# Linear attention slots: values' products earlier, features ahead of residuals and turns, scatter and sum of looked-up rows on GpSimd

## The chip, the cores and the metric

One core of a Trainium2 chip. The metric is the device time of one execution in microseconds (us). The engines are TensorE (PE; PEld is its weight load), VectorE (DVE), ScalarE (ACT), GpSimd (POOL) and SyncE (SP), each with its own instruction stream; they meet at semaphores. SP and GpSimd also issue the DMAs that are spoken of here.

## The reference, cut to what matters

A block of six residual layers on 4 x 512 tokens of width 512. The first three are of interest, the kernel weaves them:

```python
x = x + 0.5 * L0_ffn(layernorm(x))      # looked-up spline rows: route, look up, scatter, sum
x = x + L0_attn(layernorm(x))           # linear attention with sine features
x = x + 0.5 * L0_ffn(layernorm(x))
# then two Hadamard feed-forwards around a differential attention
# L0_attn:
q, k = rotate(h @ Wq.T + bq), rotate(h @ Wk.T + bk); v = h @ Wv.T + bv
qp = concat(sin(p), cos(p)) / sqrt(F),  p = (q / |q|) @ R.T      # kp likewise, of k
kv = einsum('bhsf,bhsd->bsfd', kp, v)   # per token, summed over heads
out = einsum('bhsf,bsfd->bhsd', qp, kv);  return out @ Wo.T + bo
# L0_ffn, after routing a token to one of 64 tiles of 8 columns:
delta = (b + s * x_local) * output_scale[tile]
out = zeros.at[n, cols of tile].set(delta);  return x + out
```

The scatter is computed as one-hot (64 tiles) times delta (8 numbers), both broadcast to 512 columns, and then added to x.

## The kernel before

The tokens are cut into four chunks of 512 rows (4 tiles of 128). Products are made of pairs of f16 (high and low parts), three matmuls per contraction block. After the weights are set up, the kernel runs five **slots**, i = -1 to 3 (b_tensor L1290, b_scalar L1474, b_pool L1577, b_sync L1631, b_vector L1658). In slot i three chunks are in work at once (b_roles): `now` = i has its scores, weighted sums, output product and residual; `new` = i + 1 gets projections, rotation, lengths, features and values; `look` = i + 2 gets its looked-up rows, its norm and its turned rows; `back` = i - 1 is routed for the third layer. There is no planner: the order on each engine is the program's order, written by hand.

A slot has a **loop** of 17 steps (y = 0 to 16) and a **tail**. In the loop TensorE makes score(y) (L1310) and weighted(y - 1) (L1323), with the mask by the vector engine between (L1667). At fixed steps it also makes the projections of `new` (QK_AT), the lengths' sums (L1342), the turned features (L1352, steps 14 and 15) and the look-up of `look` (L1267). The vector engine does the rotation (L1685), the look-up's arithmetic, at step 12 the scaling of the rows (L1847), at 13 the scatter (L1853), at 14 the refine of the inverse root of the lengths (L1697 to L1699), at 14 also the sum (L1113), at 15 the statistics of the next norm (L2079). GpSimd does the sums and squares of the rotation (L1585, L1589). weighted(y) waits for mask(y), and mask(y) stands behind whatever the vector engine has before it.

The tail makes, for `new`, spread(a) (L1362, a copy of it on ScalarE at L1498), angle(z) (L1709, L1713, L1714), the Sin and its high part (L1504, L1507) and the low part (L1721), for z = 0 to 5. Between these stand the values' products (L1195 with 256 columns, evicted at L1740), the norm's root and rows of `look` (L2097, L2121), its turned rows (L1904, L1912, L1919), and the output products of `now` with their residuals (L1729), then, in slots 1 and 2, the routing (L447 to L479).

The features have to be laid anew, heads and features over the partitions, for the next slot's scores. They go through DRAM: SP stores the high parts pair by pair (L1602) and loads them again (L1609), GpSimd does the same for the low parts (b_low_spread, the same two lines), each waiting for a pair's store to land before its load. SP also stores the values (L1648) and loads them in eight DMAs (L1653), between the second and third pair. score(0) of the next slot waits for all of the features and for the values to be evicted; weighted(0) waits for the eight loads. The buffers of features and values are single.

Of the kernel before, what the change touches and what calls it, by code (L numbers as in the profile page):

```python
# [88 lines left out]
b_reduced b_feat b_f_hi b_f_lo b_hi_out b_lo_out b_ks b_ks2 b_ksg b_qs b_qs2 b_s b_mask b_pv b_ot_hi b_ot_lo b_out b_res b_bo  # L89
# [1132 lines left out]
QK_AT = (0, 1, 3, 4, 6, 7)  # L1222
TURN_AT = (14, 15)
# [4 lines left out]
LOOK_SCALE, LOOK_SCATTER, LOOK_ADD, LOOK_NORM = 12, 13, 14, 15  # L1228
# [61 lines left out]
def b_tensor(k, pe, i):  # L1290
# [54 lines left out]
    def turned(a):  # L1345
        pe.wait_ge(s["b_rot"], 6 * new + 2 * a + 2)
        if a == 0:
            pe.wait_ge(s["b_rope"], 6 * (new + 1))
        else:
            need(pe, s["b_y"], 3 * new + a - 1)  # L1350
# [13 lines left out]
    def output(u):  # L1364
# [4 lines left out]
        if u < 2 and new is not None:  # L1369
            pe.wait_ge(s["b_v_in"], TPC * new + u + 3)  # L1370
# [6 lines left out]
    def value(u):  # L1377
        if new is None:
            return
        if u >= 2:  # L1380
            pe.wait_ge(s["b_v_in"], TPC * new + u - 1)
        cols = slice(u * P, (u + 1) * P)
        pairs_product(pe, k.ps[:, ROWS_OUT[u % 2], 0:256], [of(h, cols) for h in ht],
                      [of(w, slice(768, 1024)) for w in w0]).then_inc(s["b_v_done"], 1)

    for y in range(PAIRS + 1):
        if now is not None:
            if y < PAIRS:
                score(y)
            if y:  # L1390
                weighted(y - 1)
        if new is not None:
            if y in QK_AT:
                project(QK_AT.index(y))
            if y in LENGTH_AT:
                length(LENGTH_AT.index(y))
            if y in TURN_AT:
# [76 lines left out]
def b_scalar(k, e, i):  # L1474
# [46 lines left out]
    for y in range(PAIRS + 1):  # L1521
        if now is not None and y and y % 4 == 0:
            sums(y // 4 - 1)
        if new is not None and y == SPREAD_AT + 1:
            inverse()
        if look is not None and y == LOOK_START + 1:
            apply_scalar(k, e, look, 1, LOOK_BANK)
        if look is not None and y == LOOK_NORM + 1:
            use_log(e)
            norm_root_scalar(k, e, look)  # L1530
# [15 lines left out]
    spread(0)  # L1546
    feature(0)
    if look is not None:
        norm_write_scalar(k, e, look, look, k.h, range(2), s["n_h"])
    spread(1)  # L1550
    feature(1)
    if look is not None:
        norm_write_scalar(k, e, look, look, k.h, range(2, TPC), s["n_h"])
    feature(2)
    spread(2)
    feature(3)
    if look is not None:
        turn_scalar(k, e, look, 0, NEXT_TURN[0])
    feature(4)
    if look is not None:  # L1560
        turn_scalar(k, e, look, 1, NEXT_TURN[1])
    feature(5)
    keys(0)
    if look is not None:
        turn_scalar(k, e, look, 2, NEXT_TURN[2])
# [1422 lines left out]
```

## Time and profile before

| | |
|---|---|
| runs of the kernel (us) | 2229.55, 2238.29, 2240.41; median 2238.29 |
| profiled execution (us) | 2230.0, of which 2228.2 from first to last instruction |
| busy: PE, DVE, ACT, POOL | 87%, 57%, 32%, 11% |
| mean granted TensorE clock | 0.932 of full speed |
| the five slots | about 237 to 636 us |
| first score of slots 0 to 3 | 317.98, 411.12, 509.13, 594.68 us |
| first Sin of slots -1 to 2 | 286.17, 379.31, 477.01, 563.23 us |

The page cuts the span into 40 slices of 55.7 us; the slots are slices 5 to 12. Matmul idleness is worth reading by what ended it, since an idle stretch of an engine that nothing waits for costs nothing.

### The profile page before, as it was taken

The page shows a single profiled execution, that of the slowest core. Times are in us where ns is not written, and L with a number is a line of the kernel's source. Part 1 is how long each engine was busy: PE and PEld are TensorE (multiplying, and loading weights), DVE is VectorE, ACT ScalarE, POOL GpSimd, SP SyncE. Part 2 cuts the span into 40 slices and gives each one's busy share as a digit, 9 for nine tenths or more (in the row PEclk, how much of TensorE's full clock was granted, in tenths as well). Part 3 has the DMA queues.
Part 4 walks back from the last instruction along what each step waited for, and adds up shares of the span by engine and source line. Part 5 has one row for each costly group of instructions (what it writes and reads, how often), then busy time and mean ns, then how long its engine had stood idle before and what let it go on. Part 6 is the DMA issues. An engine that isn't in the chain of part 4 may idle for free.

```text
span 2228.2 us, 28781 instructions
## 1 busy us (share of the span) xinstructions
PE 1943.6 (87%) x11782; PEld 925.8 (42%) x11782; DVE 1259.0 (57%) x2312; ACT 720.2 (32%) x1109; POOL 246.1 (11%) x200
## 2 busy tenths in 40 slices
PE   3876668787664999899999999999999999999999
PEld 2443334343342444344444444444444444444444
DVE  5776658578756564636674456635664456533332
ACT  3553133343322133222353224522353224412211
POOL 1830212213100000000000100000000100000000
PEclk7887879889776999999999999999999999999999
DMA  7223240330412123211120211111020211132321
GB/s 258 97 62 110 87 90 20 71 73 18 90 76 96 67 105 114 94 67 40 37 76 30 72 52 49 57 57 39 29 76 29 76 48 58 48 112 97 123 96 66
DMA packets 92457, 164.93 MB, mean 74 GB/s; under 512 B 44134, under 2 KB 55718, under 8 KB 87718
## 3 DMA queue, kind: packets, MB, share of 16 engines
q1 hardware_dynamic: 89446, 156.79, 21.8%
q0 software_dynamic: 2880, 6.31, 1.2%
q8 instruction: 93, 1.52, 0.3%
q14 instruction: 38, 0.31, 0.0%
HBM read 137.89 MB, written 25.17 MB: 73 GB/s over the span
## 4 chain that ended last, share of the span: by engine, by line
PE 50%; DVE 4%; ACT 2%; issue 1%; ACTq 0%; DVEq 0%
PE ps L1195 27%; PE ps L1989 12%; PE ps L2503 2%; PE ps L2522 1%; DVE arena L2667 1%; PE ps L2499 1%; PE ps L2505 1%; PE ps L2449 1%; PE ps L2540 1%; PE ps L2524 1%; PE ps L2526 1%; PE ps L2529 1%; PE ps L2531 1%; PE ps L2446 1%; DVE arena L2044 0%
## 5 line engine op out<-in xcount | busy, mean ns | idle before, releaser
L1195 PE MATMUL ps<-arena 128*128 128x512 f16 (+1 forms) x4512 | 1010.1, 379 | 22.9 <-DVE arena L2044 12.8
L1195 PEld LDWEIGHTS ps<-arena 128*128 128x128 f16 x4512 | 434.0, 98 | 529.9 <-issue 28.4
L1989 PE MATMUL ps<-arena 128*128 128x512 f16 x1536 | 343.8, 379 | 12.5 <-DVE arena L2072 9.3
L1989 PEld LDWEIGHTS ps<-arena 128*128 128x128 f16 x1536 | 146.6, 97 | 185.8 <-DVE arena L2072 12.1
L2044 DVE SCALAR_TENSOR_TENSOR arena<-arena,ps 128x512 f32<-128x512 f32 x128 | 87.8, 686 | 208.5 <-ACT arena L2011 207.9
L2011 ACT ACTIVATE arena<-ps,arena 128x512 f32<-128x512 f32 x128 | 87.7, 685 | 358.6 <-PE ps L1195 358.4
L2596 ACT ACTIVATE arena<-ps 128x1024 f32<-128x1024 f32 (+3 forms) x128 | 90.2, 705 | 254.4 <-PE ps L2505 254.4
L2701 DVE CAST arena<-arena 128x1024 f16<-128x1024 f32 (+3 forms) x128 | 66.2, 517 | 150.6 <-ACT arena L2596 148.6
L2667 DVE TENSOR_REDUCE arena<-ps 128x2 f32<-128x256 f32 (+3 forms) x128 | 99.5, 819 | 65.1 <-PE ps L2449 65.1
L2072 DVE SCALAR_TENSOR_TENSOR arena<-ps,arena 128x512 f32<-128x512 f32 x64 | 44.0, 687 | 134.5 <-PE ps L1989 134.3
L2053 DVE SCALAR_TENSOR_TENSOR arena<-ps,arena 128x512 f32<-128x512 f32 x128 | 95.7, 748 | 39.2 <-PE ps L1195 39.1
L2703 DVE TENSOR_TENSOR arena<-arena 128x1024 f16<-128x1024 f32 (+3 forms) x128 | 111.4, 870 | 4.4
L2647 POOL TENSOR_TENSOR arena<-arena 128x512 f16<-128x512 f32 x32 | 37.1, 1160 | 624.1 <-ACT arena L2574 624.1
L2035 DVE TENSOR_TENSOR arena<-arena 128x512 f16<-128x512 f32 x128 | 90.8, 710 | 4.0 <-ACT arena L2003 4.0
L1667 DVE TENSOR_TENSOR arena<-ps,arena 128x256 f32<-128x256 f32 x128 | 47.4, 416 | 68.8 <-PE ps L1310 68.4
L2003 ACT ACTIVATE arena<-arena 128x512 f16<-128x512 f32 x128 | 79.6, 622 | 17.5 <-DVE arena L2053 17.5
L2651 POOL TENSOR_TENSOR arena<-arena 128x512 f32<-128x512 f32 x16 | 19.0, 1187 | 581.6 <-DVE arena L2714 581.6
L741 PE MATMUL ps<-arena 128*128 128x128 f32 x240 | 45.3, 332 | 37.3 <-DVE arena L979 18.6
L2571 ACT ACTIVATE arena<-ps 128x512 f32<-128x512 f32 x32 | 19.1, 597 | 166.7 <-PE ps L1195 166.7
L2503 PE MATMUL ps<-arena 32*128 32x512 f16 (+3 forms) x768 | 72.8, 293 | 0.0
L1323 PE MATMUL ps<-arena 128*32 128x64 f32 x1024 | 41.9, 294 | 33.2 <-DVE arena L1667 32.8
L1904 PE MATMUL ps<-arena 128*128 128x128 f32 x192 | 30.1, 303 | 43.9 <-ACT arena L2121 40.2
(270 smaller groups left out, 2342.4 us busy)
## 6 DMA issues: line engine op xcount, KB each, us to landing
arena<-wug_dram SPq DMA_DIRECT2D x128, 512.0 KB, 3.3
arena<-wd_hi_dram SPq DMA_DIRECT2D x16, 1024.0 KB, 5.0
arena<-wd_lo_dram SPq DMA_DIRECT2D x16, 1024.0 KB, 7.2
wug_dram<-arena SPq DMA_DIRECT2D x4, 2048.0 KB, 16.1
arena<-feat_dram SPq DMA_DIRECT2D x24, 256.0 KB, 4.7
arena<-_attn_hidden_states_dram SPq DMA_DIRECT2D x4, 1024.0 KB, 15.9
arena<-in_L_ffn_W_up_dram SPq DMA_DIRECT2D x8, 512.0 KB
arena<-in_L_ffn_W_down_dram SPq DMA_DIRECT2D x4, 1024.0 KB, 7.2
```

The costliest lines, as they stand in the source:

```text
L1195: ins = pe.matmul(out, left[a](c), right[b](c), start=(at == 0), stop=(at == 3 * n - 1))
L1989: ins = pe.matmul(k.ps[:, bank, :], act[x][:, slot, cols], wd[y][:, f, :], start=(f == 0 and m == 0), stop=(f == 7 and m == 2))
L2003: e.activation(k.act_hi[:, g % ACT_SLOTS, :], k.prod[:, g % 2, :], ACT.Copy).then_inc(s["f_hi"], 1)
L2011: e.activation(k.th[:, g % 2, :], k.ps[:, GATE_BANK, :], ACT.Tanh, scale=k.wscale[:, FB + a:FB + a + 1])\
L2035: e.tensor_tensor(k.act_lo[:, g % ACT_SLOTS, :], k.prod[:, g % 2, :], k.act_hi[:, g % ACT_SLOTS, :], ALU.subtract)\
L2044: e.scalar_tensor_tensor(out=th, in0=th, scalar=1.0, in1=k.ps[:, GATE_BANK, :], op0=ALU.add, op1=ALU.mult)\
L2053: e.scalar_tensor_tensor(out=k.prod[:, g % 2, :], in0=k.ps[:, UP_HALF_BANK, :], scalar=k.wscale[:, a:a + 1], in1=th, op0=ALU.mult, op1=ALU ...
L2503: pe.matmul(k.ps[:, bank, queries], x[rows, 4 + b, keys], y[rows, b, queries], start=False, stop=False)
L2596: e.activation(k.p32[:, t % 2, :, queries], k.ps[:, 0:2, queries], ACT.Exp, scale=SCORE).then_inc(s["c_exp"], 1)
L2667: e.tensor_reduce(k.mx[:, u, 4 * b + 2 * j:4 * b + 2 * j + 2], k.ps[:, bank:bank + 2, 0:(u + 1) * P], AXX, ALU.max).then_inc(s["c_max"], 1)
L2701: e.tensor_copy(k.p_hi[:, t % 2, :, queries], k.p32[:, t % 2, :, queries]).then_inc(s["c_p_hi"], 1)
L2703: e.tensor_tensor(k.p_lo[:, t % 2, :, queries], k.p32[:, t % 2, :, queries], k.p_hi[:, t % 2, :, queries], ALU.subtract).then_inc(s["c_p_l ...
```

## The change

Five edits, all in the slots:

- the values' products and evictions are made at steps 9 to 12 of the loop, in the banks of the projections, no longer in the tail; turned(0) and turned(1), in the same banks, wait for the evictions;
- SP stores and loads the values ahead of the features. The eight loads still wait for the last weighted sum;
- spread(0) is issued at step 16, before the last weighted sum, and angle(0), angle(1) at step 16 before the last low half of the sums; in the tail the features and their low parts come before residuals and turns, and ScalarE's rows and turns move behind later features; in slot -1 the norm of `look` comes wholly after the features;
- the log table is loaded once, at step 13;
- scatter and sum of `look` go to GpSimd: it waits for the scaled rows (l_scaled), makes four scatters and four sums; the vector engine waits for each sum (l_added) before its statistics, which are now at step 16, ahead of angle(0).

```diff
+VALUE_AT = (9, 10, 11, 12)
-LOOK_SCALE, LOOK_SCATTER, LOOK_ADD, LOOK_NORM = 12, 13, 14, 15
+LOOK_SCALE, LOOK_NORM = 12, 16
@@ b_tensor
-            pe.wait_ge(s["b_v_in"], TPC * (now + 1))
@@ turned
-        if a == 0:
-            pe.wait_ge(s["b_rope"], 6 * (new + 1))
+        if a < 2:
+            pe.wait_ge(s["b_v_in"], TPC * new + a + 3)
@@ loop
+            elif new is not None:
+                spread(0)
             if y:
                 weighted(y - 1)
+            if y in VALUE_AT:
+                value(VALUE_AT.index(y))
@@ tail
-        spread(0)
-    value(0)
-    value(1)
-    if new is not None:
+        if now is None:
+            spread(0)
         spread(1)
-    value(2)
-    value(3)
-    if new is not None:
+        turned(2)
         spread(2)
-        turned(2)
@@ b_scalar, loop and tail
+        if now is not None and y == PAIRS:
+            spread(0)
         if new is not None and y == SPREAD_AT + 1:
+            use_log(e)
             inverse()
...
+    if ahead:
+        norm_root_scalar(k, e, look)
     feature(0)
-    norm_write_scalar(... range(2) ...)
     spread(1)
     feature(1)
-    norm_write_scalar(... range(2, TPC) ...)
+    if ahead:
+        next_rows(range(2))
+    spread(2)
     feature(2)
-    spread(2)
+    if ahead:
+        next_rows(range(2, TPC))
     feature(3)
     feature(4)
     feature(5)
+    if ahead:
+        next_turns(range(2))
+    elif look is not None:
+        use_log(e)
+        norm_root_scalar(k, e, look)
+        next_rows(range(TPC))
+        next_turns(range(2))
     keys(0)
@@ b_pool, behind the rotation's sums and squares
+        if look is not None:
+            e.wait_ge(s["l_scaled"], look)
+            for u in range(TPC):
+                e.tensor_tensor(k.scat[:, u, :].rearrange("p (t j) -> p t j", j=DSL),
+                                bcast(k.oh4[:, u, :].unsqueeze(2), [P, NTILE, DSL]),
+                                bcast(k.ap[3][:, u, :].unsqueeze(1), [P, NTILE, DSL]), ALU.mult).then_inc(s["l_added"], 1)
+            for u in range(TPC):
+                e.wait_ge(s["l_added"], 8 * (look - 1) + u + 1)
+                xt = k.x[:, look * TPC + u, :]
+                e.tensor_tensor(xt, xt, k.scat[:, u, :], ALU.add).then_inc(s["l_added"], 1)
@@ b_sync: ahead of the features
+    sp.wait_ge(s["b_v_in"], TPC * (i + 1))
+    sp.dma_start(scratch.rearrange("(u p) n -> p u n", p=P), k.v0).then_inc(s["b_v_out"], 16)
+    need(sp, s["b_pv"], PAIRS * i)
+    sp.wait_ge(s["b_v_out"], 16 * (i + 1))
+    for h in range(8):
+        sp.dma_start(k.vr[...], scratch[:, 32 * h:32 * h + 32]...).then_inc(s["b_vr"], 16)
@@ b_vector, loop
+            if y - 1 in VALUE_AT:
+                value(VALUE_AT.index(y - 1))
             if y == LOOK_SCALE:
                 scale_start_vector(k, V, look)
                 scale_tiles_vector(k, V, look, range(TPC))
-            if y == LOOK_SCATTER:
-                e.wait_ge(s["b_rot"], 6 * (new + 1))
-                for u in range(TPC):
-                    scatter_tile_vector(k, V, u)
-            if y == LOOK_ADD:
-                add_sum_vector(k, V, look)
-            if y == LOOK_NORM:
-                norm_sums_vector(k, V, look, range(TPC))
-                norm_spread_vector(k, V)
+                e.sem_inc(s["l_scaled"], 1)
+            if y == LOOK_NORM and now is not None:
+                next_sums()
+        if now is not None and y == PAIRS:
+            angle(0)
+            angle(1)
@@ b_vector, tail
+    if look is not None and now is not None:
         norm_refine_vector(k, V, look)
-    angle(0); value(0); angle(1); value(1); low(0); angle(2); low(1); value(2); angle(3); value(3)
-    low(2); angle(4); low(3); turned(0); angle(5); residual(0); turned(1); low(4); residual(1)
-    low(5); turned(2); turned(3); residual(2); residual(3)
+    low(0); angle(2); low(1); angle(3); low(2); angle(4); low(3); angle(5); low(4); low(5)
+    if look is not None and now is None:
+        next_sums()
+        norm_refine_vector(k, V, look)
+    residual(0); turned(0); residual(1); turned(1); turned(2); turned(3); residual(2); residual(3)
```

The last hunk is written one statement after the other on a line to keep it short; next_sums waits for each sum and takes that tile's statistics, and then their spread.

## Rows read from the trace of the kernel before

**Rows 1.** Busy us and instructions of each engine, clock, DMA; slot 0
```profile
318.00:411.00 93.00, 70.82 (x530) 34.39 (x530) 62.35 (x133) 28.85 (x41) 23.68 (x25) 0.89 0.27 55
```
**Rows 2.** Timeline of matmuls (start, us, count, idle before): first scores, last routing of slot 1
```profile
317.98 0.58 PE L1310 MATMUL ps<-arena 96*128 96x256 f16 x2 [17.79 <-DMA arena<-feat_dram]
...
411.12 0.58 PE L1310 MATMUL ps<-arena 96*128 96x256 f16 x2 [12.47 <-DMA arena<-feat_dram]
...
505.30 1.79 PE L479 MATMUL ps<-arena 64*128 64x16 f32 x8 [0.68 <-ACT arena L498]
509.13 0.58 PE L1310 MATMUL ps<-arena 96*128 96x256 f16 x2 [2.04 <-DMA arena<-feat_dram]
...
594.68 1.01 PE L1310 MATMUL ps<-arena 96*128 96x256 f16 x4 [5.59 <-DMA arena<-feat_dram]
```
**Rows 3.** Timeline of GpSimd, hand-off behind slot 0
```profile
385.49 0.60 POOL L1602 DMA_DIRECT2D feat_dram<-arena  x1 [2.56 <-DVE arena L1721]
388.97 0.61 POOL L1609 DMA_DIRECT2D arena<-feat_dram  x1 [2.88 <-DMA feat_dram<-arena]
...
396.79 0.59 POOL L1609 DMA_DIRECT2D arena<-feat_dram  x1 [5.82 <-DMA feat_dram<-arena]
...
405.33 0.60 POOL L1609 DMA_DIRECT2D arena<-feat_dram  x1 [6.76 <-DMA feat_dram<-arena]
```
**Rows 4.** Timelines of the vector engine and ScalarE, end of slot 0's loop and its tail
```profile
364.35 2.87 DVE L1853 TENSOR_TENSOR arena<-arena 128x512 f32<-128x512 f32 x4
...
369.95 2.27 DVE L1113 TENSOR_TENSOR arena<-arena 128x2048 f32<-128x2048 f32 x1
...
372.93 2.46 DVE L2079 BATCH_NORM_STATS2 arena<-arena 128x6 f32<-128x512 f32 x4
...
377.40 0.69 DVE L1709 SCALAR_TENSOR_TENSOR arena<-ps,arena 128x512 f32<-128x512 f32 x1
...
384.49 0.68 DVE L1721 SCALAR_TENSOR_TENSOR arena<-arena 128x512 f16<-128x512 f32 x1
...
379.31 0.72 ACT L1504 ACTIVATE arena<-arena 128x512 f32<-128x512 f32 x1 [1.04 <-DVE arena L1714]
```
**Rows 5.** Timeline of SP's DMA issues: the values' eight loads, slot 0
```profile
394.39 8.71 SPq L1653 DMA_DIRECT2D arena<-values_dram  x8
```
**Rows 6.** Windows as rows 1, in slot 0's hand-off; then queues' share, 378 to 413
```profile
386.00:394.00 8.00, 7.36 (x42) 3.92 (x40) 7.90 (x15) 5.96 (x10) 2.05 (x4) 1.00 0.87 230
...
398.00:404.00 6.00, 0.65 (x3) 0.10 (x1) 0.95 (x2) 2.94 (x3) 0.57 (x1) 0.92 1.08 163
...
q1 hardware_dynamic: 7200, 3.41, 51.8%
q0 software_dynamic: 720, 1.58, 19.0%
```
**Rows 7.** Timelines: two products on the vector engine, each with what GpSimd ran then
```profile
73.10 2.21 DVE L517 TENSOR_TENSOR arena<-arena 128x512 f32<-128x512 f32 x1
...
72.42 2.34 POOL L697 TENSOR_TENSOR arena<-arena 128x1024 f32<-128x1024 f32 x1
...
504.19 4.63 DVE L517 TENSOR_TENSOR arena<-arena 128x512 f32<-128x512 f32 x1
...
504.04 4.22 POOL L1595 TENSOR_TENSOR arena<-arena 128x512 f32<-128x512 f32 x4
```
**Rows 8.** Instructions grouped by line and form, whole span: busy us, mean ns
```profile
L696 POOL TENSOR_TENSOR arena<-arena 128x1024 f32<-128x1024 f32 x16 | 38.4, 2400 | 72.9 <-ACT arena L853 71.9
L1585 POOL TENSOR_TENSOR arena<-arena 128x512 f32<-128x512 f32 x24 | 31.2, 1320 | 180.7 <-DVE arena L1685 180.7
L1595 POOL TENSOR_TENSOR arena<-arena 128x512 f32<-128x512 f32 x16 | 17.0, 1092 | 51.3 <-DVE arena L1729 51.2
...
L1740 DVE SCALAR_TENSOR_TENSOR arena<-ps,arena 128x256 f32<-128x256 f32 x16 | 6.7, 417 | 0.0
```
**Rows 9.** Timeline of matmuls: one pair of values' products, slot 0
```profile
374.69 2.79 PE L1195 MATMUL ps<-arena 128*128 128x256 f16 x24
```

More of the change, by code:

```diff
@@ L1368, in output @@
             pe.wait_ge(s["b_ot_lo"], TPC * (now + 1))
-        if u < 2 and new is not None:
-            pe.wait_ge(s["b_v_in"], TPC * new + u + 3)
         if u >= 2:
@@ L1377, in value @@
     def value(u):
-        if new is None:
-            return
-        if u >= 2:
+        if u < 2:
+            pe.wait_ge(s["b_rope"], 6 * new + 5 + u)
+        else:
             pe.wait_ge(s["b_v_in"], TPC * new + u - 1)
         cols = slice(u * P, (u + 1) * P)
-        pairs_product(pe, k.ps[:, ROWS_OUT[u % 2], 0:256], [of(h, cols) for h in ht],
+        pairs_product(pe, k.ps[:, PROJ_BANK[u % 2], 0:256], [of(h, cols) for h in ht],
                       [of(w, slice(768, 1024)) for w in w0]).then_inc(s["b_v_done"], 1)
@@ L1545, in b_scalar, with next_rows, next_turns @@
     body = back is not None and new is not None
-    spread(0)
+    def next_rows(tiles):
+        norm_write_scalar(k, e, look, look, k.h, tiles, s["n_h"])
+    def next_turns(cols):
+        for c in cols:
+            turn_scalar(k, e, look, c, NEXT_TURN[c])
+    ahead = look is not None and now is not None
+    if ahead:
+        norm_root_scalar(k, e, look)
+    if now is None:
+        spread(0)
     feature(0)
-    if look is not None:
-        norm_write_scalar(k, e, look, look, k.h, range(2), s["n_h"])
     spread(1)
     feature(1)
-    if look is not None:
-        norm_write_scalar(k, e, look, look, k.h, range(2, TPC), s["n_h"])
+    if ahead:
+        next_rows(range(2))
+    spread(2)
     feature(2)
-    spread(2)
+    if ahead:
+        next_rows(range(2, TPC))
     feature(3)
-    if look is not None:
-        turn_scalar(k, e, look, 0, NEXT_TURN[0])
     feature(4)
-    if look is not None:
-        turn_scalar(k, e, look, 1, NEXT_TURN[1])
     feature(5)
+    if ahead:
[5 more added lines that the diff above has]
+        next_turns(range(2))
     keys(0)
     if look is not None:
-        turn_scalar(k, e, look, 2, NEXT_TURN[2])
-        turn_scalar(k, e, look, 3, NEXT_TURN[3])
+        next_turns(range(2, KC))
     keys(1)
@@ L1739, in value, with next_sums @@
         e.wait_ge(s["b_v_done"], TPC * new + u + 1)
-        e.scalar_tensor_tensor(out=k.v0[:, u, :], in0=k.ps[:, ROWS_OUT[u % 2], 0:256], scalar=1.0 / (W_SCALE * A_SCALE),
+        e.scalar_tensor_tensor(out=k.v0[:, u, :], in0=k.ps[:, PROJ_BANK[u % 2], 0:256], scalar=1.0 / (W_SCALE * A_SCALE),
                                in1=k.bv, op0=ALU.mult, op1=ALU.add).then_inc(s["b_v_in"], 1)
+    def next_sums():
+        for u in range(TPC):
+            e.wait_ge(s["l_added"], 8 * (look - 1) + 4 + u + 1)
+            norm_sums_vector(k, V, look, (u,))
+        norm_spread_vector(k, V)
     for y in range(PAIRS + 1):
@@ L1796, in b_vector, with turned @@
     body = back is not None and new is not None
-    turned = (lambda c: turn_vector(k, e, look, c, NEXT_TURN[c])) if look is not None else (lambda c: None)
-    if look is not None:
+    def turned(c):
+        if look is not None:
+            turn_vector(k, e, look, c, NEXT_TURN[c])
+    if now is None:
+        angle(0)
+        angle(1)
+    if look is not None and now is not None:
         norm_refine_vector(k, V, look)
-    angle(0)
-    value(0)
-    angle(1)
-    value(1)
     low(0)
@@ L1812, in b_vector @@
     low(3)
+    angle(5)
+    low(4)
+    low(5)
+    if look is not None and now is None:
+        next_sums()
+        norm_refine_vector(k, V, look)
+    residual(0)
     turned(0)
-    angle(5)
-    residual(0)
+    residual(1)
     turned(1)
-    low(4)
-    residual(1)
-    low(5)
     turned(2)
@@ L2839, in _ @@
         def _(pool):
+            use_splines(k, k.work, k.work[:, 2048:4096])
+            use_look(k)
             setup_pool(k, pool)
```

25 lines of the change are left out of this document (7 added, 18 removed).

## The prediction

> **What bounds the kernel now.** I read the page's forty slices first: TensorE is at 6 to 9 tenths until slice 16 and at 9 from there, and nothing of the diff runs after that. The change lives in the five slots of the linear attention, some 237 to 636 us. The matmul timeline of that stretch shows the engine mostly full inside a slot and then standing idle in front of the next slot's first score: 17.79, 12.47, 2.04 and 5.59 us, 37.9 us in four waits, each ended by a DMA out of feat_dram [rows 2]. A whole slot's window says the same: 70.82 us of matmuls in 93 us [rows 1]. In slot 1 the wait is short only because the routing's matmuls end at 507.1, just before the DMA [rows 2]. So the hand-off (features, stores, loads, score) is what the change can shorten; the rest is a matter of order.
>
> What is in a hand-off (slot 0): the vector engine adds the looked-up rows in one piece (2.27 us), takes the statistics (2.46 us from 372.93), refines, and only then forms the first angle at 377.40; the first Sin starts at 379.31 [rows 4]. I call that start t; it is 286.17, 379.31, 477.01 and 563.23 in slots -1 to 2, four rows of one pattern. From t the score is 31.8, 31.8, 32.1 and 31.5 us away. GpSimd's queue carries that distance: the second low part ends at 385.17 (t + 5.9), its store issues at 385.49, the load follows at 388.97, two stores wait till 396.79, two more till 405.33, and the last load lands at 411.1 [rows 3, 4]. The low parts are ready long before the queue comes to them. The waits for landings are 5.8 and 6.8 us because the DMA engines are full: share 0.87 and then 1.08 [rows 6], with the values' store and their eight loads in the middle (issued from 394.39 for 8.71 us) [rows 5].
>
> **Part by part.**
>
> Values' products move from behind the slot to steps 9 to 12. 48 matmuls of 256 columns, 5.6 us (2.79 for 24) [rows 9], and four evictions of 0.42 us [rows 8], leave the tail and enter the loop. In slots 0 and 1 the loop there waits for the vector engine's masks (1.96, 1.24, 3.34 us of idleness seen between 350 and 365 in slot 0), so most of it is absorbed; by adding the products step by step to the times of slot 0 I get the scale of the rows done about 2.2 us later than 363.04, at 365.2. In slot 2 the loop is fuller: idleness of 0.95, 1.69 and 0.78 us takes up about half, and t moves 2.1 us later.
>
> The values' traffic moves. The store to DRAM goes out inside the loop, when DMA is idle, and the eight loads go out at the last weighted sum (slot -1: earlier still) instead of amid the features. They are now ahead of the high parts on SP's queue: 8.7 us of issuing from about 373 ends at about 382, where the first pair of high parts is done at 382 to 384, so little waits. SP's own chain (pairs at t + 3.2, t + 9.2, t + 12.3, landings of 3.5 to 4.7 us) ends near t + 26 and is not last. What it frees: the packets of a hand-off take 51.8% and 19.0% of 35 us, 24.8 us [rows 6]; the values are 1 MB of its 5 MB, 5 us by bytes, and more by packets, since they come in short pieces. Ends: nothing (the landings are latency), and 8.7 us (the whole stretch in which they are issued). The nearest row is the first low store, which waited under 3 us while DMA was not yet full [rows 3], against 5.8 and 6.8 later. I take 4 us per slot.
>
> Features ahead of residuals and turns. ACT's row writes no longer stand in front of the second feature, the vector engine has no values' evictions and turns between the low parts. The second low part goes from t + 5.9 to t + 5.2, the fourth from t + 10.6 to t + 9.9: 0.7 us (slot 2: 0.5). The row writes end at t + 7.9 instead of t + 5.9, but the engine's outputs then start where they did, since 385.5 was set by the values. Behind them the last turn is at about t + 18 as before and the routing at about t + 30, which is where slot 1 stays: its gain is 2.0 us, not 4.7.
>
> Log table loaded once ahead of the lengths: three loads of 1.28 us become one, ahead of a refine that waited for them only in slot 2. Nothing, at most 1 us.
>
> Scatter and sum to GpSimd. The vector engine gives away 2.87 and 2.27 us [rows 4]. GpSimd gets eight 128x512 operations in three slots (-1, 0, 1), with no wait inside. Its rows are 1.09 to 1.32 us for that shape, the nearest; the upper bound is the 2.40 us of a 128x1024 one [rows 8]; I take 9.4 us for all eight. They run 365.3 to 374.7. Two waits are new. GpSimd's for the scaled rows has its feature stores behind it, which have nothing to send before t + 2.3, so it is free. The vector engine's for each sum, in front of the statistics, has the first two angles behind it, the last low half of the weighted sums, the norm's refine and every low part. If nothing else happened the first Sin would start at 377.8, 1.5 us earlier.
>
> But the square root's refine (three SBUF-to-SBUF operations of 24x512, 0.68 us each) falls inside that burst, and the mask of step 15 is behind it. The trace has that collision. A product of two SBUF operands took 2.21 us instead of 0.69 while a GpSimd operation of 2.34 us was running: it went in between two of them [rows 7]. Another took 4.63 us, under four GpSimd additions of 4.22 us: it got in behind the last [rows 7]. By the first pattern each refine step waits for one GpSimd operation, and GpSimd for it: refine ends 3 us later, GpSimd 2 us later, and t is 0.5 us later than before. By the second all waits until 374.7, mask, statistics and angle follow, and t is 3.1 us later. I take the first: the row stands for eight or so like it, the other is alone.
>
> The Trainium skill ("SBUF — State Buffer", Who interferes with whom) has the pair of ports of VectorE and GpSimd as an exclusive lock, held for one instruction, where the second to issue blocks until the first finishes. By that rule the delay is the first pattern's, 0.5 us; the row of 4.63 us contradicts it, since four instructions went first. The rule speaks against this part of the change in either reading.
>
> **The sum**, for the profiled execution (span 2228.2, 2230.0 in all):
> - slot -1: before, refine ended at 277.5 and the first angle began at 284.3; now only the spread and its copy lie between, 2.7 us, so 4.1 us are won. The refine's waits cost 3, and the products, which stand among waits for GpSimd on a clock that had fallen to half there, 0 to 4.5; I leave t at 286.2. The chain from t loses 1.5 us (second low part at t + 4.4), 4.0 as above, and 0.5 at the last load, as the values are wholly past: t + 25.8. The next chunk's norm now follows the features: from the statistics to the last turn the first chunk took 12.7 us (224.8 to 237.5), so t + 11.7 + 12.7 = t + 24.4, just hidden. 31.8 becomes 25.8: -6.0
> - slot 0: -0.7 - 4.0 + 0.5 = -4.2
> - slot 1: -2.0 (routing) + 0.5 = -1.5
> - slot 2: no scatter, no turns: 2.1 - 0.5 - 4.0 = -2.4
> Together -14.1. The profiled execution was one of the fast ones: 2230.0 stands against runs of 2229.55 to 2240.41 and a median of 2238.29, so the profile should show about 2216 and a median of runs about 2225.
>
> **Rivals.**
> 1. *No collision* (refine slips in, 1.5 us won at three starts, and more in slot -1): -21, time 2217. For it: masks and statistics do not suffer, since they read PSUM or one operand. Against it: the rows of rows 7.
> 2. *The whole burst blocks*: t 3.1 us later in slots 0 and 1, about 6 in slot -1: -3, time 2235. For it: the 4.63 us, whose GpSimd operations are of the very kind of the new sums.
> 3. *The hand-off is latency, not bandwidth*: landings stay at 5.8 and 6.8 us though the values are gone. Four times 4 us come back: +2, time 2240. Against: 2.9 us for the first one.
> 4. *The other side: GpSimd is slow at broadcasts.* No row shows one with a repeated operand. At the 2.4 us of twice the size, four scatters add 4.6 us; as the angles stand behind the statistics, and these behind the last sum, that goes one for one into t in three slots, 14 us, on top of case 2, whose longer burst also holds mask 15: -3 + 14 = +11, time 2249. It decides from about 2.1 us per scatter with a blocked refine.
> That the change does not do what it says: the loads of the values could not start before the last weighted sum (their buffer is single), so "first half" is true of products and store alone; this is in the sum.
>
> **How the numbers follow.** Forecast 0.45, rival 1 0.15, rival 2 0.22, rival 3 0.08, rival 4 0.10. The measurement can tell about 0.5%, 11.2 us, from no change. The forecast's own spread is some 6 us either way (the 4 us per slot has ends 0 and 7.5), so it lies beyond 11.2 in seven of ten: 0.32, with rival 1 0.15 and some of rival 2 0.03: faster 0.50. Slower: half of rival 4 and tails, 0.10. The rest is the same, 0.40. Time 2225; the range of 8 in 10 runs from beyond rival 1, whose own spread is 5 us, 2211, to just past rival 3, 2243; rival 4 and the far tails stay out.
>
> **What would show it.** Right: idleness before the four first scores down from 37.9 to about 22 us; DMA share over 1 shorter, GpSimd's two-store waits near 4.5 us; the values' loads ended before the second load of low parts; the first refine step 1.5 to 2 us long in slots 0 and 1; slot 1 unchanged but for 1 or 2 us because routing ends late. Wrong: a refine step of 6 us or more (rival 2), scatters over 2 us (rival 4), landings unchanged (rival 3), or a loop that grew by the full 5.6 us in slots 0 to 2, which would cost 9 us more.

## The result and the profile after

| | before | after |
|---|---|---|
| runs | 2234.98 us (2229.55 to 2240.41, 4 runs) | 2215.2 us (2211.1 to 2217.91, 4 runs) |
| profiled execution | 2230.0, span 2228.2 | 2216.1, span 2214.3 |

Ratio 0.9908, interval 0.9889 to 0.9927: 0.9% faster, 19.8 us. Forecast was 2225. The profile came out where the forecast put it (about 2216), the median did not. One run of x2_out_first (below) and one of the kernel before beside it took over 2900 us at a clock of 0.64, and no number here uses them.

In what follows a slot runs from first score to first score (slot -1 from the first turned rows), t is the start of the first Sin, and "slots" is the time from the first slot's start to the first matmul group of the feed-forward behind slot 3. First the matmul timeline of the changed kernel where it answers to [rows 2].

```profile
307.19 1.94 PE L1933 MATMUL ps<-arena 128*128 128x128 f32 x8 [16.34 <-ACT arena L2150]
...
311.45 0.63 PE L1310 MATMUL ps<-arena 96*128 96x256 f16 x2
...
380.32 1.94 PE L1933 MATMUL ps<-arena 128*128 128x128 f32 x8 [4.29 <-ACT arena L2150]
382.05 7.11 PE L1195 MATMUL ps<-arena 128*128 128x512 f16 x24
...
391.04 5.34 PE L1195 MATMUL ps<-arena 128*128 128x512 f16 x24
399.06 0.41 PE L1310 MATMUL ps<-arena 96*128 96x256 f16 x2 [2.68 <-issue]
...
470.43 7.29 PE L1195 MATMUL ps<-arena 128*128 128x512 f16 x24
...
491.37 1.86 PE L479 MATMUL ps<-arena 64*128 64x16 f32 x8 [0.68 <-ACT arena L498]
493.16 0.61 PE L1310 MATMUL ps<-arena 96*128 96x256 f16 x2
...
576.73 1.89 PE L479 MATMUL ps<-arena 64*128 64x16 f32 x8 [0.68 <-ACT arena L498]
578.61 1.01 PE L1310 MATMUL ps<-arena 96*128 96x256 f16 x4
```

Of the 37.9 us in front of the four first scores 2.68 are left, where about 22 were forecast. They stand at the end of slot 0; the releaser reads "issue" (none shown), but GpSimd's last load is issued at 395.41 (below) and such loads land after 3.7 us in the median, so it is still the hand-off. In two more profiles of the kernel after (below) only 0.79 and 1.18 us stand there, ended by the vector engine's last residual. The idle time has moved as well as shrunk: in slot -1 the turned rows wait 16.34 us, since their norm now follows the features, and the score comes just behind them; in slots 0 and 1 the turned rows wait 4.29 and 3.87 us, in slot 2 the output products 4.56. In slots 1 and 2 the routing's last matmuls (L479) end where the score begins: another end has taken the DMA's place there.

GpSimd behind slot 0, the columns of [rows 3], with the burst it was given:

```profile
359.47 4.64 POOL L1603 TENSOR_TENSOR arena<-arena 128x512 f32<-128x512 f32 x4 [10.52 <-DVEq L1801]
364.07 5.14 POOL L1609 TENSOR_TENSOR arena<-arena 128x512 f32<-128x512 f32 x4
376.24 0.64 POOL L1622 DMA_DIRECT2D feat_dram<-arena  x1 [7.02 <-DVE arena L1742]
...
382.24 0.60 POOL L1629 DMA_DIRECT2D arena<-feat_dram  x1 [3.39 <-DMA feat_dram<-arena]
...
388.97 0.59 POOL L1629 DMA_DIRECT2D arena<-feat_dram  x1 [4.95 <-DMA feat_dram<-arena]
...
395.41 0.60 POOL L1629 DMA_DIRECT2D arena<-feat_dram  x1 [4.66 <-DMA feat_dram<-arena]
```

The vector engine meanwhile, the collision of [rows 7] as it came out here:

```profile
361.75 1.43 DVE L1718 TENSOR_TENSOR arena<-arena 24x512 f32<-24x512 f32 x1
363.20 1.45 DVE L1719 SCALAR_TENSOR_TENSOR arena<-arena 24x512 f32<-24x512 f32 x1
364.69 1.47 DVE L1720 SCALAR_TENSOR_TENSOR arena<-arena 24x512 f32<-24x512 f32 x1
...
369.31 0.69 DVE L2108 BATCH_NORM_STATS2 arena<-arena 128x6 f32<-128x512 f32 x1 [0.36 <-POOL arena L1609]
```

Each refine step takes 1.43 to 1.47 us instead of 0.68, one GpSimd operation's wait each, and the statistics wait 0.36 us for the last sum. SP's loads of the values and the hand-off's windows, beside [rows 5] and [rows 6]:

```profile
369.56 4.70 SPq L1663 DMA_DIRECT2D arena<-values_dram  x8
```
```profile
376.00:384.00 8.00, 3.71 (x14) 2.46 (x14) 7.69 (x14) 7.34 (x12) 2.99 (x5) 0.67 0.71 168
384.00:392.00 8.00, 7.05 (x33) 3.43 (x32) 4.00 (x7) 4.14 (x8) 1.80 (x4) 0.90 0.77 203
```

DMA is no longer full (0.71 and 0.77, against 0.87 and 1.08; at equal distances from t, 8 to 16 and 16 to 24 us, it is 0.86 and 0.62 against 0.99 and 1.12), and GpSimd's two-store waits fell from 5.82 and 6.76 to 4.95 and 4.66 us.

**Several profiles of each.** One profile of before was too few: three of it and three of the kernel after give this (us, mean; t from the slot's start / from t to the next first score):

| kernel (profiles) | slot -1 | slot 0 | slot 1 | slot 2 | slots | behind them |
|---|---|---|---|---|---|---|
| before (3) | 54.2 / 31.8 | 61.4 / 31.7 | 65.9 / 32.3 | 55.8 / 31.7 | 403.3, 408.5, 406.3 | 1592.4 to 1592.6 |
| before + values (2) | 57.4 / 24.7 | 63.4 / 25.4 | 64.4 / 30.3 | 57.5 / 26.2 | 392.8, 389.9 | 1598.2, 1598.0 |
| before + GpSimd (1) | 56.3 / 32.1 | 61.3 / 30.2 | 64.8 / 32.2 | 57.0 / 30.6 | 403.9 | 1593.5 |
| after, sum on DVE (2) | 52.1 / 25.2 | 63.1 / 26.0 | 63.4 / 31.7 | 56.7 / 29.5 | 389.3, 391.0 | 1598.6, 1598.4 |
| after, SP's old order (1) | 53.0 / 30.1 | 59.4 / 30.0 | 61.8 / 32.2 | 57.3 / 30.8 | 396.3 | 1598.5 |
| after (3) | 52.5 / 24.9 | 61.0 / 25.5 | 60.7 / 32.3 | 57.4 / 28.0 | 386.8, 385.3, 382.6 | 1592.6 to 1593.7 |

The slots became 21.1 us shorter in the mean (406.0 to 384.9), which is the 20 to 23 us of the runs. The forecast's 14.1 was met only between two single executions (2230.0 and 2216.1), and by luck: the first profile of before had the shortest slots of its three, the first of after the longest of its three.

### The profile page after: what moved, and what is told of

It reads as the page before. It is cut to its first block, busy times and chain, and to the rows that moved or that the text cites. A ratio compares the mean times of both kernels' runs of the same rounds, so it can differ in the third digit from the quotient of the medians.

```text
span 2214.3 us, 28789 instructions
## 1 busy us (share of the span) xinstructions
PE 1947.4 (88%) x11782; PEld 925.7 (42%) x11782; DVE 1254.1 (57%) x2297; ACT 716.2 (32%) x1105; POOL 275.5 (12%) x224
## 4 chain that ended last, share of the span: by engine, by line
PE 50%; DVE 4%; ACT 2%; issue 1%; ACTq 0%; DVEq 0%
PE ps L1195 27%; PE ps L2018 12%; PE ps L2532 2%; PE ps L2551 1%; DVE arena L2696 1%; PE ps L2528 1%; PE ps L2534 1%; PE ps L2478 1%; PE ps L2569 1%; PE ps L2553 1%; PE ps L2555 1%; PE ps L2560 1%; PE ps L2558 1%; PE ps L2475 1%; DVE arena L2073 0%
## 5 line engine op out<-in xcount | busy, mean ns | idle before, releaser
L2082 DVE SCALAR_TENSOR_TENSOR arena<-ps,arena 128x512 f32<-128x512 f32 x128 | 95.8, 748 | 39.5 <-PE ps L1195 39.1
L1323 PE MATMUL ps<-arena 128*32 128x64 f32 x1024 | 41.8, 292 | 26.3 <-DVE arena L1688 26.2
## 6 DMA issues: line engine op xcount, KB each, us to landing
arena<-_attn_hidden_states_dram SPq DMA_DIRECT2D x4, 1024.0 KB, 16.9
```

What stands on the lines that cost most here:

```text
L2082: e.scalar_tensor_tensor(out=k.prod[:, g % 2, :], in0=k.ps[:, UP_HALF_BANK, :], scalar=k.wscale[:, a:a + 1], in1=th, op0=ALU.mult, op1=ALU ...
```

## Experiments

Ratios are to the kernel before, run beside; its median was about 2234.2 us. "Over the kernel after" means over c0_after's 2210.78 us; against the 2215.2 us of the first result every such difference is 4.4 us smaller. Where an experiment has one profile, its slots are of one execution.

**c0_after: the kernel after, unchanged.**

> The changed kernel itself, again. Theory A (the two profiled executions are typical): it comes out 14 us (0.6%) below the kernel before, as the profiles 2230.0 and 2216.1 do. Theory B (the kernel before has slower executions that the changed one does not have, since its hand-offs were at the limit of DMA): 20 us (0.9%) below, with a smaller spread from run to run than the kernel before.

2210.78 us, 0.9891 [0.9869, 0.9913]: 23 us below, with runs 3.8 us apart against 15.3 for the kernel before, so theory B, if anything by more than its 20 us. A third profile (c0b_after) had slots of 382.6 us where 385 to 387 were expected.

**b0_before and b0c_before: the kernel before, twice more.**

> The kernel before once more, for a second profile of it. What is asked is where its executions of 2229 to 2244 us differ. Theory P (the clock's returns to full speed outside the slots come at other moments of the work from run to run): slots within 3 us of 403.3, feed-forwards and last attention between 1592 and 1599 us, with the difference where the granted clock rises at 700 to 720 us or falls at 930 and 1160. Theory Q (the hand-offs themselves vary): the difference is inside the slots.

> The kernel before once more, for what one profile of it is worth. Its first profile had slots of 403.3 us in all (start of the first slot to the first feed-forward matmul), its second 408.5 us, with the same 1592.4 and 1592.5 us behind them. Theory A (the under-forecast is mostly that the first profile was a fast execution): slots of 405 to 411 us, with the first Sin of slot 2 at 56 to 57.5 us from the slot's start as in the second profile, not 54.1. Rival B (the step of each slot was mis-sized): slots of 402 to 405 us, and the second profile is the odd one. On what lies behind the slots, theory P (by execution) expects either 1592 to 1594 or 1598.5, theory K (by kernel) expects 1592.5 again.

Slots of 408.5 and 406.3 us, t of slot 2 at 57.1 and 56.3 us: theory A. Behind them it is 1592.5 and 1592.6 us, so the executions differ inside the slots (theory Q). The execution on which the sum was built was some 3 us short in the slots, most of it in slot 2.

**b1_values: the first two edits alone.**

```diff
 (kernel before, the edit in words)
+    value(u) at steps 9 to 12 on TensorE and the vector engine
+    SP: store and loads of the values ahead of the features
```

> The kernel before with one part alone: values' products and evictions at steps 9 to 12 and their store and loads ahead of the features on SP; the tail's order, the tables and the scatter stay. Theory 1 (DMA relief is the larger part, 4 us in each of four hand-offs, and the products are absorbed by the loop): 12 to 14 us faster than before. Theory 2 (the order of the tail and the chain's start is what counts): at most 5 us faster. In the trace by theory 1 GpSimd's waits for two stores fall from 5.8 and 6.8 us to under 5.

2221.69 us, 0.9938 [0.9918, 0.9959]. From t to the score 5.5 to 7.1 us less in slots -1, 0 and 2, 2 us less in slot 1; t is 3.2 us later in slot -1 and 2.0 in slot 0. The slots are 14.7 us shorter than before, two thirds of the whole change, and GpSimd's waits for two stores are 3.88 and 3.55 us in slot 0: theory 1.

**b2_pool: scatter and sum on GpSimd alone.**

> The kernel before with scatter and sum of looked-up rows on GpSimd alone, the statistics still at step 15, tail and values as before. Theory 1 (refine is held one GpSimd operation per step, statistics wait for the last sum): t moves by +0.5 to +1.5 us in three slots, 2 to 4 us slower than before. Rival (freeing the vector engine of 5.1 us per slot helps the masks): 3 to 6 us faster.

2235.11 us, 1.0001 [0.9986, 1.0016]. Nothing, neither forecast. The slots of its one profile, 403.9 us, lie within before's own 403.3 to 408.5.

**c2_dve_scatter: the kernel after with scatter and sum back on the vector engine.**

```diff
-                e.sem_inc(s["l_scaled"], 1)
+            if y == LOOK_SCALE + 1:
+                ... scatter_tile_vector(k, V, u)
+            if y == LOOK_SCALE + 2:
+                add_sum_vector(k, V, look)
```

> The changed kernel with scatter and sum back on the vector engine at steps 13 and 14, statistics at step 16 as in the changed kernel. If GpSimd's burst costs what it frees (theory 1): within 3 us of the changed kernel. If the move pays: 4 to 8 us slower than the changed kernel, about 1.3 to 2.7 per slot. If it costs: 2 to 4 us faster.

2219.73 us, 0.9928 [0.9907, 0.995]; a second profile much the same. t is 2.1 and 2.7 us later in slots 0 and 1 than in the kernel after. So GpSimd's part is worth nothing alone and 5 us of slots on top of the other parts. From the first weighted sum to t it takes off 1.2 and 1.3 us in slots 0 and 1 alone (b2), 2.4 and 2.4 here: the parts interact. That the evictions fill the engine that GpSimd relieves would explain it, but no run shows that; in b2 the statistics also stand at step 15 and not at 16.

**c1_sp_old: the kernel after with SP's order of before.**

> The changed kernel with SP's order of before: the values' store between the features' second and third pair and the eight loads behind it; products, tail and GpSimd's part as changed. Theory 1 (the values' traffic in the full stretch of the hand-off cost about 4 us each): 8 to 14 us slower than the changed kernel, GpSimd's waits for two stores back near 5 to 7 us, a DMA again in front of the first scores of slots 0, 1 and 3. Rival (the chain would be as short without it, the gain is from products and order): under 3 us slower.

2226.72 us, 0.9972 [0.9958, 0.9986]: 16 us over the kernel after by medians, 11 in the slots, the other 5 behind them. From t to the score 5.2, 4.5, 0 and 2.8 us more, and GpSimd's waits go back up:

```profile
386.40 0.61 POOL L1629 DMA_DIRECT2D arena<-feat_dram  x1 [3.95 <-DMA feat_dram<-arena]
...
393.72 0.60 POOL L1629 DMA_DIRECT2D arena<-feat_dram  x1 [5.53 <-DMA feat_dram<-arena]
```

The forecast's 4 us for the values' traffic is borne out in three of the four slots (slot 1 has another end), and with 12 us it is the largest single piece.

**c3_tail_old: the kernel after with the old order of tail and norm.**

> The changed kernel with the tail's old order: ScalarE's rows and turns between the features, the vector engine's residuals and turns between the low parts, and in slot -1 the norm ahead of the features. My sum (0.7 us per hand-off, and 7 us of statistics and norm in slot -1): 4 to 9 us slower than the changed kernel, most of it in slot -1, and in slot 1 nothing or a gain, since TensorE's outputs need not wait for the rows and the clock stays up. Rival (features first is worth 3 us in every slot): 10 to 13 us slower.

2217.28 us, 0.9937 [0.9917, 0.9957]. t of slot -1 is 5.5 us later than in the kernel after (forecast of that step: 4.1). Slots 0 to 2 are 0.9 to 1.4 us shorter than in the kernel after: there the new tail brings nothing. In all its slots take 385.9 us against 384.9, so the whole reordering of the tail is worth about 1 us there; most of the 6.5 us over the kernel after stands behind the slots (1598.5 us).

**x1_scatter_early: GpSimd's scatters released at step 11 instead of 12, to end the burst before the refine.**

> The changed kernel with GpSimd's four scatters released when the looked-up values are done (step 11) and only the sums behind the scaled rows. The burst then ends about 5 us earlier, and the statistics have nothing to wait for; the refine still meets one or two sums. If the wait for the last sum and the held refine set the first Sin: t 1.5 to 2.5 us earlier in slots 0 and 1, 3 to 4 us faster in all. Rival (the scaling of the rows is now the one that is held, four operations of 0.5 us behind scatters of 1.1): no gain, as the scaling ends 2 to 4 us later.

2221.69 us, 0.9951 [0.9935, 0.9967]: 11 us over the kernel after, 5 of them in the slots; the rival came. The wait for the last sum went, but the collision only moved: three small steps of the scale's arithmetic (128x4) took 0.47, 1.00 and 1.00 us, and two refine steps still 1.47 and 1.46.

**c4_after_refine: the burst released behind the refine.**

```diff
+                if look is not None:
+                    e.wait_ge(s["b_r"], new + 1)
+                    e.sem_inc(s["l_scaled"], 1)
-                e.sem_inc(s["l_scaled"], 1)
```

> The changed kernel with GpSimd's scatters and sums released only behind the square root's refine (step 14) instead of behind the scaled rows (step 12). The three refine operations no longer meet GpSimd's and take 0.68 us each instead of 1.45, but the burst of 9 us starts 5 us later in slots 0 and 1. Theory 1 (the statistics wait for the last sum and the first angle for the statistics): t 3 to 4 us later in slots 0 and 1, about 5 us slower. Rival (held refine is the costly part): 2 to 4 us faster.

2225.12 us, 0.9958 [0.9939, 0.9977]. The refine is at 0.67, 0.68, 0.68 us again, and the price appears at the statistics, in slot 1:

```profile
460.15 0.69 DVE L2110 BATCH_NORM_STATS2 arena<-arena 128x6 f32<-128x512 f32 x1 [4.44 <-POOL arena L1609]
```

The wait stands before the first angle; TensorE waits 5.49 us for that angle (in front of L1352) and then takes 3.75 us for four matmuls that took 1.99 at full clock just before; slot 1 takes 97.5 us instead of 93.0. t is 1.2 and 5.2 us later in slots 0 and 1 (3 to 4 were expected), and in slot -1, where the burst now ends at 286.5, it is 4.3 us longer from t to the score. The slots are 11 us longer in all: the 2.3 us of collision are the cheaper of the two.

**x2_out_first and x6_slot1_slot2: the outputs ahead of the turned rows**, in slots 0 and 1, then in slot 1 alone with residuals ahead of low(5) in slot 2.

> The changed kernel with TensorE's first two output products ahead of the first two sets of turns in slots 0 and 1. In the changed kernel TensorE stands 4.3 and 3.9 us idle for the norm's rows, the granted clock falls to half and the two outputs take 7.1 to 7.3 us instead of 5.3. Theory C (that idleness and clock are what holds slot 1 to 32.3 us from the first Sin to the score, where 30.1 were forecast): slot 1 gains 1.5 to 3 us, slot 0, which the DMA ends, at most 1: 2 to 4 us faster than the changed kernel. Rival (the turns are then late and the last of them ends the hand-off): no gain or 1 to 2 us slower.

2214.95 us, 0.9924 [0.9902, 0.9947], 4 us over the kernel after: no gain, the rival. From t to the score slot 1 gains 1.3 us, but the idle time moves to the turned rows (4.64 us in slot 0).

> The changed kernel with two edits: output products ahead of the turns in slot 1 alone, and in slot 2 the vector engine's first two residuals ahead of the last two low parts, so that TensorE does not stand 4.5 us idle for them. Slot 1 gained 1.3 us from the first Sin to the score in the run with both slots' outputs moved. In slot 2 the score comes right behind the routing's last matmul, so it should gain 2 to 3 us unless the DMA is there only a little earlier (GpSimd's last load is issued at 573.7 and lands in 4 us, the score is at 578.6): then nothing. In all 1 to 4 us faster, or the same if the clock falls elsewhere.

x6, two profiles: slots of 379.6 and 383.0 us, 3.7 less than after in the mean, but 1598.2 us behind them both times; 2211.21 us, 0.9888 [0.9868, 0.9908], so no faster than the kernel after.

**What stands behind the slots (x6b, c2b, b1b: second profiles).**

> The kernel with outputs first in slot 1 and residuals early in slot 2, a second profile. Its first had slots of 379.7 us, 5 us less than the kernel after, and 1598.2 us behind them, so that no gain was left. Theory P: slots of 379 to 381 again and, at an even chance, 1592 to 1594 behind them, total about 2205. Theory K: 1598.2 again, total 2209 to 2211.

> The kernel after with scatter and sum on the vector engine, a second profile. Its first had 389.3 us of slots and 1598.6 us behind them, the kernel after 382.6 to 386.8 and 1592.6 to 1593.7. Theory P (the 5 us behind the slots are by execution, so that GpSimd's part is worth only the 4 us of the slots): about an even chance of 1592 to 1594. Theory K (they are by kernel: where the slots end decides where the clock stands at fixed places behind them, so that the part is worth 9 us here): 1598.5 again, to 0.3 us.

A second profile of b1 had slots of 389.9 us, less than the 392 to 396 expected, and 1598.0 us behind them. Over 20 profiles it is 1592.4 to 1594.0 us or 1598.0 to 1598.7 us, with the same work, and it goes with the kernel: before and after are three times in three at the low value, b1, c2 and x6 twice in two at the high one (theory K). For executions without a profile that is not shown: c2's six runs lie at 2215.3 and 2215.9 us and at 2219.6 to 2222.3, as if two had gone the other way. Between the second profile of c2 and the third of the kernel after the difference has grown to 1.4, 2.9, 4.1 and 5.7 us by 35, 125, 314 and 572 us behind the slots. The third of these four steps is this, the same 48 matmuls behind the same idle time, 13.25 and 12.07 us.

```profile
922.26 13.25 PE L1195 MATMUL ps<-arena 128*128 128x512 f16 x48 [3.64 <-DVE arena L2067]
```
```profile
912.71 12.07 PE L1195 MATMUL ps<-arena 128*128 128x512 f16 x48 [3.65 <-DVE arena L2073]
```

The granted clock is at 1.2 GHz for the first matmuls of both (0.50 over the first 3 us) and comes back to 2.4 GHz later in one (0.59 against 0.98 over the next 3 us). Why it does so in one kernel and not in another stays open. So of the 9 us by which c2 is slower than the kernel after only the 5 in the slots can be put down to GpSimd's part, and x6's gain is undone behind the slots.

**d1_quarter and d2_double: does the moved work hold slot 1's clock?**

```diff
-                      [of(w, slice(768, 1024)) for w in w0]).then_inc(s["b_v_done"], 1)
+                      [of(w, slice(768, 1024)) for w in w0],
+                      n=KC if now is None else 1).then_inc(s["b_v_done"], 1)
```

> The kernel after, with the values' products of slots 0, 1 and 2 cut to their first contraction block (3 of 12 matmuls each, so its values are not those of the reference): 36 matmuls of 256 columns, about 4.2 us of TensorE at full clock, leave each of the three loops at steps 9 to 12; evictions and all waits stay. Theory C (these products fill idle stretches and keep the granted clock up in the second half of slot 1's loop, which is why the first Sin of slot 1 came 5 us earlier than before and not 0.5 us later): with most of them gone the granted clock in slot 1's loop from 36 to 54 us after its first score falls below 0.8 again, and the first Sin of slot 1 is at 63 to 66 us from the slot's start (60.1 to 61.8 in the kernel after), although there is less to do; total within 4 us of the kernel after on either side. Rival D (the products cost what they are, and the gain in slot 1 is of another part): the clock stays where it is, each t comes 0 to 2 us earlier (slot 2 most), total 2 to 8 us shorter.

> The kernel after, with each value's product of slots 0, 1 and 2 made twice into the same bank (48 more matmuls of 256 columns and 5.6 us of TensorE per slot at full clock; the result is the same). Theory C: the loops of slots 0 and 1 take most of it in idle stretches and stay at full clock: first Sin 0 to 2.5 us later in slots 0 and 1, 3 to 5.6 us later in slot 2, total 4 to 10 us longer. Rival D: what is added is paid in full, 15 to 17 us longer.

Windows of 18 us, from 36 us after slot 1's first score, columns as in [rows 1]: before, after (third profile), d1.

```profile
447.00:465.00 18.00, 12.58 (x103) 5.93 (x104) 13.01 (x31) 4.42 (x5) 3.43 (x4) 0.61 0.00 1
```
```profile
431.00:449.00 18.00, 15.18 (x151) 8.44 (x144) 13.90 (x30) 3.14 (x4) 7.46 (x7) 0.91 0.09 30
```
```profile
429.90:447.90 18.00, 14.22 (x111) 6.58 (x113) 13.01 (x29) 3.14 (x4) 6.56 (x6) 0.72 0.08 29
```

d1: 2218.66 us, 0.9918 [0.9886, 0.9951], no shorter than the kernel after though 36 matmuls, 4.2 us, are gone from each of three slots. The clock does fall (0.72 against 0.91), as theory C says, but t of slot 1 is at 61.1, not at 63 to 66: the part of C that matters, that the clock of this stretch made the 5 us, is not borne out. From the first weighted sum to t slot 1 is 0.9 us longer than in the kernel after, slot 0 is 1.0 shorter. The single profile was the shortest of d1's four runs (2209.26), so its slots can't be compared closer. d2: 2225.73 us, 0.9957 [0.9939, 0.9975], 15 us over the kernel after by ratios, 9 by slots, between the two theories; t is 3.0 to 3.5 us later in each of slots 0 to 2. From the first weighted sum to t the first dose of 5.6 us costs 1.2, 0.4 and 1.6 us in slots 0, 1 and 2 (b1), the second costs 3.0, 2.4 and 3.9: the loops take in most of the first and about half of the second.

## Why the prediction was right in its direction and too small

The step that failed is t in slot 1: the forecast put its first Sin 0.5 us later, and it came 5.3 us earlier. Against the mean of three profiles each, forecast / measured in us:

| | t from the slot's start | from t to the score |
|---|---|---|
| slot -1 | 0 / -1.7 | -6.0 / -6.9 |
| slot 0 | +0.5 / -0.4 | -4.7 / -6.3 |
| slot 1 | +0.5 / -5.3 | -2.0 / 0.0 |
| slot 2 | +2.1 / +1.5 | -4.5 / -3.8 |
| sum | +3.1 / -5.8 | -17.2 / -16.9 |

The matmul timelines divide t further, at the first weighted sum (L1323), means in us, before / after:

| | first score to first weighted sum | first weighted sum to t |
|---|---|---|
| slot 0 | 4.7 / 6.6 | 56.7 / 54.4 |
| slot 1 | 5.9 / 3.7 | 60.1 / 57.0 |
| slot 2 | 5.2 / 5.6 | 50.7 / 51.8 |
| slot 3 | 1.5 / 3.7 | 39.6 / 39.1, to the slot's end |

- **What bounds it: right.** The hand-offs were the place; the waits for feat_dram in front of the four scores are gone and the sum from t to the score came out within 0.3 us, though its single terms are off by 0.7 to 2.0 and cancel.
- **The values' traffic (4 us per slot, taken between 0 and 8.7): right.** c1 shows 5.2, 4.5, 0, 2.8, one profile.
- **Slot 1's -2.0 (routing at t + 30.1): wrong, 0.0.** The step was "the engine's outputs then start where they did, since 385.5 was set by the values". They did not: in the kernel after TensorE stands idle for 4.29 us (slot 0) and 3.87 us (slot 1) before the turned rows at t + 7.9, and the first pair of outputs runs at the lower clock for it, 7.11 and 7.29 us instead of 5.34. What was moved away had filled the time in which the rows are written. x6, with outputs there instead, has the score at t + 29.6 and t + 29.9 in its two profiles.
- **The collision: right in pattern and size.** Three refine steps held for one GpSimd operation each, 2.3 us (forecast 3), burst 9.7 us (forecast 9.4). The Trainium skill ("SBUF — State Buffer", Who interferes with whom) has a lock per instruction; these rows agree with it, and neither rival 2 nor rival 4 came (scatters 4.64 us for four). x1 and c4 moved the burst, and neither place was cheaper. But the other pattern, the 4.63 us, was not alone as the prediction had it. In all three profiles of before a routing product (L517) that meets GpSimd's four residual additions is held to the end of the last, 4.63, 4.03 and 4.82 us, and in all three of after, 3.45, 2.77 and 2.81 us instead of 0.69. Why the additions hold it through and the burst does not stays open.
- **t in slot 1: the step that failed.** Forecast +0.5, measured -5.3. The forecast charged the products 2.2 us, as in slot 0, took 1.7 back for scatter, sum and angles with the collision, and put the start of the slot at nothing. The start made 2.2 of the 5.3 us. Between score(0) and weighted(0) TensorE makes the first projection, 12 matmuls. Before, it had stood idle for 12.0 to 12.7 us ahead of the score, the granted clock was 0.50, and they took 5.16 to 5.32 us. After, with 0.8 to 2.7 us idle, the clock is 1.00 ahead of the score, and they take 2.76 us in two profiles and 4.44 in one. Here before and c0_after:

```profile
411.50 5.32 PE L1195 MATMUL ps<-arena 128*128 128x512 f16 x12
```
```profile
397.38 2.76 PE L1195 MATMUL ps<-arena 128*128 128x512 f16 x12
```

So the shorter hand-off pays a second time, and b1 alone has 1.9 us of this. The other 3.1 us lie behind the first weighted sum, by part: the products +0.4 (b1) instead of +2.2, and tail with angles at step 16 -1.1 (c2) and GpSimd's part -2.4 (after against c2), 3.5 together, instead of 1.7. Slot 0 has +1.2, -1.1 and -2.4 there. The clock of the loop's second half, 0.61 before and 0.91 after, is the lesser part: an estimate from d1 (0.72 there, slot 1 0.9 us longer where slot 0 is 1.0 shorter) is 1 to 2 us. What in the loop of slot 1 takes in the products better than slot 0's is not shown.
- **The norm "just hidden" in slot -1: 2 us late.** Forecast for the last turn was t + 24.4. The turned rows are complete only at t + 26.3 to t + 27.0, where slot 0's first projection, which waits for them, begins, 1.6 us behind the score instead of 0.4. It then takes 4.8 us instead of 4.1, at a granted clock of 0.56 instead of 0.66. That is slot 0's start, +1.9 us, which eats what the loop and the angles won there (t -0.4).

```profile
313.07 4.86 PE L1195 MATMUL ps<-arena 128*128 128x512 f16 x12 [0.99 <-DVE arena L1948]
```

- **t in slot -1: -1.7 instead of 0.** The norm behind the features gives 5.5 us (c3; forecast 4.1), the products cost 3.2 (b1; forecast 0 to 4.5, taken as 1.1, since t was left at 0), and GpSimd's burst 0.4 (after against c2; forecast 3).
- **Slot 3: 0 / +1.6** (41.2 to 42.7), not in the forecast. It is in the slot's start, 1.5 to 3.7 us: the score comes sooner, the vector engine is still at the routing, whose product is held by GpSimd's residual additions as said above, and mask(0) stands behind it. The kernel after, vector engine and TensorE:

```profile
575.62 3.45 DVE L517 TENSOR_TENSOR arena<-arena 128x512 f32<-128x512 f32 x1
```
```profile
582.67 0.66 PE L1323 MATMUL ps<-arena 128*32 128x64 f32 x16 [3.05 <-DVE arena L1688]
```

- **From profile to median: wrong.** I added 8.3 us to both kernels, the distance of one profile from a median of three runs. Over 17 runs of before the median is 2234.2, not 2238.3, and the kernel after had no such distance: its profile was 2216.1 and its median 2215.2. Of the miss of 9.8 us (2225 to 2215.2) 3.3 are the base (2238.3 against the 2235.0 of the result) and 6.5 the change itself, 13.3 forecast and 19.8 measured; in the slots it was 14.1 forecast and 21.1 measured, and the 7 us between are the terms of t and slot 3 above. The agreement of the two profiles hid this.

## What to carry to other kernels

- Before a sum is made on one profile, ask where that execution stands among the runs; here it was 3 us short in the very slots that were changed, and the offset to the median was not a property of the kernel.
- Take traffic that can go earlier out of a stretch in which DMA is full, also if its bytes are few: 1 MB of 5 was worth 12 us over four hand-offs.
- When a wait is shortened, follow the engine into its next product: here the first projection behind the wait ran at full clock and gave 2.2 us more in slot 1, and work that was put behind the hand-off took 1.9 us back in slot 0.
- Before work is moved away from an engine, look at what it was covering. And test parts together: GpSimd's part was worth 0 alone and 5 us with the values' part.

## What the runs showed of the hardware that was not expected

- Identical work behind the changed region differs by 4.0 to 6.3 us between two groups of kernels and by at most 1.1 us between profiles of one kernel. In the place looked at closely, 1.2 us of it, TensorE's granted clock returns later (13.25 against 12.07 us for 48 matmuls). A comparison below 0.3% can be made of this alone.
- A vector product with two SBUF operands was held over as many as four GpSimd additions, in six profiles of six (2.77 to 4.82 us instead of 0.69), though it is let in after one operation of the burst.
- Small vector operations are held like large ones: 128x4 steps took 1.00 us instead of 0.17 under GpSimd's burst, as a 24x512 step took 1.45 instead of 0.68.
- A GpSimd product with both operands broadcast costs what a plain addition does: four of 128x512 took 4.19 us in slots 0 and 1 of c4, beside no vector operation with two SBUF operands, and four residual additions 4.23 us in the kernel after.
